# A vision tower's convolution loop with its first activations stored four patches interleaved

## What is computed

```python
x = (x - mean) / (1e-06 + std) / math.sqrt(P)        # per patch and colour
x = _conv2d(x, conv1_w, conv1_b)                     # 3 -> 64 channels, 3x3
residual = x
x = gelu(_group_norm(x, gn1_g, gn1_b))               # 32 groups of 2 channels
x = _conv2d(x, rconv1_w, rconv1_b)                   # 64 -> 64, 3x3
x = gelu(_group_norm(x, gn2_g, gn2_b))
x = _conv2d(x, rconv2_w, rconv2_b)                   # 64 -> 64, 3x3
x = residual + x
x = _conv2d(x, proj_w, proj_b, stride=P, pad=0)      # one token of 192 per patch
```

## Time and profile before

| | us |
|---|---|
| time, median of 3 runs (lowest, highest) | 1486.84 (1485.9, 1489.83) |
| time of the profiled execution | 1486.23 |
| its span | 1484.4 |
| PE busy in it | 1367.0 (92%) |
| DVE busy | 1098.0 (74%) |
| ACT busy | 860.0 (58%) |
| POOL busy | 582.6 (39%) |

### The profile page before, as it was taken

The page is one execution under the profiler, slowest core; times in us unless marked ns, Lnnn a source line. Parts: engine busy times, 40 slices in busy tenths (PEclk is TensorE's granted clock), DMA queues, the critical chain, the costliest instruction groups (busy, mean ns, idle before and its releaser), DMA issues. The chain is left out here.

```text
span 1484.4 us, 43767 instructions
## 1 busy us (share of the span) xinstructions
PE 1367.0 (92%) x14042; PEld 1005.5 (68%) x14042; DVE 1098.0 (74%) x4148; ACT 860.0 (58%) x2126; POOL 582.6 (39%) x1116
## 2 busy tenths in 40 slices
PE   3999988888999999999999998999999977998889
PEld 1865543334888588768977875789588867754647
DVE  4763358999888988888898888888888864545520
ACT  1333337777767776666776766676767630343451
POOL 1000035555554544455455444455454420152600
PEclk9999999999999999999999999999999988898999
DMA  7899845544555555455545554555455579300000
GB/s 209 237 270 267 242 117 160 179 123 128 147 140 134 138 139 147 119 137 146 140 118 156 136 146 104 146 147 139 123 149 139 145 219 259 79 1 1 2 0 17
DMA packets 125141, 205.78 MB, mean 139 GB/s; under 512 B 20028, under 2 KB 88188, under 8 KB 124478
## 3 DMA queue, kind: packets, MB, share of 16 engines
q1 hardware_dynamic: 124990, 203.71, 50.3%
HBM read 103.11 MB, written 20.70 MB: 83 GB/s over the span
## 5 line engine op out<-in xcount | busy, mean ns | idle before, releaser
L629 PE MATMUL rc<-sb_acts,sb_rwd 128*64 128x512 f16 x1764 | 561.5, 391 | 21.4 <-DMA sb_acts<-sb_hst 21.2
L630 PE MATMUL rc<-sb_acts,sb_rwd 128*64 128x512 f16 x1764 | 562.3, 392 | 0.0
L481 POOL TENSOR_TENSOR sb_tmp<-sb_mst,sb_half_neg 128x8 f32<-128x8 f32 x200 | 353.6, 1768 | 463.8 <-DVE sb_mst L956 463.8
L548 ACT ACTIVATE sb_f32q<-c,sb_gsh,sb_gsc 128x128 f32<-128x128 f32 x792 | 298.3, 458 | 274.5 <-POOL sb_gsh L491 274.5
L629 PE MATMUL rc<-sb_acts,sb_rwl 128*64 128x512 f16 x1176 | 362.6, 390 | 5.3 <-issue 5.3
L630 PE MATMUL rc<-sb_acts,sb_rwl 128*64 128x512 f16 x1176 | 362.0, 390 | 0.0
L720 PE MATMUL pj_st<-sb_wall_arena 128*64 128x384 f16 x1792 | 304.0, 333 | 6.6 <-DVE sb_wall_arena L975 6.6
L568 ACT ACTIVATE sb_g2f<-rc,sb_gsh,sb_gsc 128x128 f32<-128x128 f32 x784 | 297.3, 481 | 4.6 <-POOL sb_gsh L491 4.6
L724 PEld LDWEIGHTS pj_st<-sb_wall_arena 128*64 128x64 f16 x1792 | 220.9, 222 | 65.8
L724 PE MATMUL pj_st<-sb_wall_arena 128*64 128x192 f16 x1792 | 240.9, 245 | 0.0
L629 PEld LDWEIGHTS rc<-sb_acts,sb_rwd 128*64 128x64 f16 x1764 | 179.1, 110 | 84.2 <-DMA sb_acts<-sb_hst 33.2
(11 more groups left out here) (190 smaller groups left out, 1864.0 us busy)
## 6 DMA issues: line engine op xcount, KB each, us to landing
sb_acts<-sb_hst SPq DMA_DIRECT2D x792, 78.8 KB, 2.6
sb_im<-x_planes SPq DMA_DIRECT2D x202, 136.5 KB
sb_wall_arena<-w_lo SPq DMA_DIRECT2D x48, 528.0 KB, 3.8
sb_acts<-sb_hst SPq DMA_DIRECT2D x96, 162.0 KB, 3.2
sb_wall_arena<-w_lo SPq DMA_DIRECT2D x24, 480.0 KB, 3.7
sb_f32q<-in_proj SPq DMA_DIRECT2D x12, 576.0 KB, 4.6
sb_wall_arena<-in_proj SPq DMA_DIRECT2D x12, 576.0 KB, 4.6
w_lo<-sb_wall_arena SPq DMA_DIRECT2D x8, 768.0 KB, 3.7
```

The lines of the kernel that those rows point to most:

```text
L481: ch.did(gp.tensor_tensor(t1, var, half_neg[:, :], ALU.pow))
L548: ins = nc.scalar.activation(g1f[:, q * Q + m, :], c1[q][:, m * HALF:(m + 1) * HALF], ACT.Gelu, bias=gsh[q][:, m:m + 1], scale=gsc[q][:, m ...
L629: nc.tensor.matmul(out[0:CH, :], w_odd, x_odd, start=(n == 0), stop=(n == 14))
L630: yield nc.tensor.matmul(out[CH:128, :], w_even, x_even, start=(n == 0), stop=(n == 14))
```

## The change

The four patches of a half are interleaved in `hst` and in `acts`: number by number, four patches side by side, rows of 18 x 4 numbers, as the weight stage has it for channels. A pair's moving operand becomes 8 runs of 64 contiguous numbers, and the shift `m` is four elements. The matmul's output in PSUM then has the patches interleaved as well, so `bn_stats` and `gelu2` of `rc` read every fourth number of a bank (a step of 16 bytes); conv1's input and output stay as they were. `split1` writes its two results with a step of four float16 numbers (8 bytes). The four copies of `double` leave out one zero row of 72 numbers in place of one of 18, so a partition copies 576 numbers (1152 bytes) and not 630 (1260 bytes). `rows_zeroed` clears rows of 72 in place of 18, once. A plane of `acts` grows from 1314 to 1368 numbers (2628 to 2736 bytes), which moves planes 1 and 2 in the weight stage too.

No instruction is added or taken away, and none changes its place on its engine.

```diff
-HB = U * PAD + WD
+HB = U * PAD + WD * Q
@@ double (SP)
-                    sp.dma_start(acts[p][64 * half:64 * half + 64, row, q * Q * PAD + WD:(q + 1) * Q * PAD],
-                                 hst[q][64 * row:64 * row + 64, WD:Q * PAD]).then_inc(s_dup[p][q], 16)
+                    sp.dma_start(acts[p][64 * half:64 * half + 64, row, q * Q * PAD + WD * Q:(q + 1) * Q * PAD],
+                                 hst[q][64 * row:64 * row + 64, WD * Q:Q * PAD]).then_inc(s_dup[p][q], 16)
@@ gelu2_at (ACT)
-                    ins = nc.scalar.activation(g2f[:, q * Q + m, :], rc[p][q][:, m * HALF:(m + 1) * HALF], ACT.Gelu,
+                    ins = nc.scalar.activation(g2f[:, q * Q + m, :], rc[p][q][:, :].rearrange("p (n g) -> p g n", g=Q)[:, m, :], ACT.Gelu,
@@ pairs (PE)
-                    return bass.AP(tensor=buf, offset=k * HB + (q * Q * SL + slot) * WD + m,
-                                   ap=[[3 * HB, 128], [PAD, Q], [WD, 8], [1, P]])
+                    return bass.AP(tensor=buf, offset=k * HB + q * Q * PAD + (slot * WD + m) * Q,
+                                   ap=[[3 * HB, 128], [WD * Q, 8], [1, P * Q]])
@@ rows_zeroed (DVE)
-                    v.memset(t[:, 0:2, q * Q * PAD:q * Q * PAD + WD], 0.0).then_inc(s_rowz, 1)
+                    v.memset(t[:, 0:2, q * Q * PAD:q * Q * PAD + WD * Q], 0.0).then_inc(s_rowz, 1)
@@ channel_stats (DVE)
+                patch = src[:, :].rearrange("p (n g) -> p g n", g=Q) if at else src[:, :].rearrange("p (g n) -> p g n", g=Q)
                 for m in range(Q):
-                    v.bn_stats(bn6[s][:, at + m, :], src[:, m * HALF:(m + 1) * HALF]).then_inc(s_dch, 1)
+                    v.bn_stats(bn6[s][:, at + m, :], patch[:, m, :]).then_inc(s_dch, 1)
@@ split1 (DVE)
-                hi = hst[q][:, :].rearrange("p (g r w) -> p g r w", g=Q, r=SL)[:, :, 1:9, 1:17]
-                lo = acts[p][:, 2, q * Q * PAD:(q + 1) * Q * PAD].rearrange("p (g r w) -> p g r w", g=Q, r=SL)[:, :, 1:9, 1:17]
+                hi = hst[q][:, :].rearrange("p (r w g) -> p g r w", g=Q, r=SL)[:, :, 1:9, 1:17]
+                lo = acts[p][:, 2, q * Q * PAD:(q + 1) * Q * PAD].rearrange("p (r w g) -> p g r w", g=Q, r=SL)[:, :, 1:9, 1:17]
```

## The result

The changed kernel takes 1626.36 us (median of 4 runs, 1622.65 to 1631.04) where the kernel before takes 1486.37 (4 runs on the same chip, 1483.55 to 1489.83): a ratio of **1.093, 95% interval 1.0907 to 1.0952**. It is slower by 140 us; the forecast was 1461.5, the range ended at 1486.

The account below looks back on a forecast made before the run. PE was taken to bound the 144 slots with projection, a ring through DVE, POOL, ACT, DMA and PE the other 52. Terms -21.6 - 2 - 1.5 + 0.5 = -24.6 us took 1486.2 to 1461.5 us, range 1453 to 1486.

Parts of the forecast that it names:

- the 144 slots: Loop slots with projection: PE bounds them at 5.07 us, so a cheaper matmul is worth its full saving there.
- DVE's own slot: Time DVE would need for a loop slot if it waited for nothing: about 4.65 us.
- the other 52: Slots without projection, 4.80 us each: cheaper matmuls worth little (2 us in all), dearer DVE instructions their full cost.
- the ring through five engines: Slots without projection: held by a chain of waits through DVE, POOL, ACT, DMA and PE.
- Part 1, the matmuls: PE's matmuls of pairs: 0.15 us saved a slot (0.10 to 0.19), 21.6 us over 144 slots, mainly from removing odd starts.
- The sum made of it: Whole kernel: -21.6 - 2 - 1.5 + 0.5 = -24.6 us, from 1486.2 to 1461.5 us.
- Two small terms: Further savings: 2 us (0 to 5) in the 52 slots without projection, 1.5 us (0 to 2) in the weight stage.
- with the ends of part 1 alone: Total if only the matmul saving takes its bounds (14.4 to 27 us): stated as 1471 to 1453 us.
- Part 2, DVE: Six DVE instructions a slot get a step: bn_stats stays 283 ns, L966 425, L968 696, no cost.
- The slower rival: PSUM step halves bn_stats' pace: DVE's slot 5.18 us, total 1528 us; chance 0.09 for bn_stats or L968 slower.
- Its last sentence: In split1's TENSOR_TENSOR: the same end, 1528 us, would come if L968's step cost 1.0 ns an element.
- The L966 rival: split1's CAST loses its pace, 0.27 us more: DVE's slot 4.92, 52 slots pay 14 us, total about 1485; chance 0.13.

Follow-up runs that it names:

- e3: The changed kernel with split1 reading and writing contiguously on all sides, values landing at wrong pixels: 1472.25 us, ratio 0.989 to the kernel before.
- e10: The kernel before, with pairs of m = 1 reading where m = 0 reads, so every run starts at an even number: 1478.24 us, ratio 0.991.
- e5: The changed kernel with only split1's CAST writing stepped, its TENSOR_TENSOR contiguous on all sides: 1514.19 us (the kernel before 1491.24).

## Why the prediction was wrong

**The bound.** Right for the 144 slots, and it was the useful part: PE bounds them, DVE's own slot is 4.65 us, and DVE counts as soon as it grows. 4.65 + 1.11 gives the slot that came. For the other 52 the ring through five engines was only part of the story. A slot of group 0 in the kernel before, in which DVE waits for no other engine:

```profile
271.70 0.43 DVE L966 CAST sb_hst<-sb_f32q 128x512 f16<-128x512 f32 x1
...
275.84 0.18 DVE L951 TENSOR_REDUCE sb_mst<-pj_st 128x16 f32<-128x32 f32 x1
...
276.37 0.43 DVE L966 CAST sb_hst<-sb_f32q 128x512 f16<-128x512 f32 x1
```

It takes 4.67 us, the median of group 0; 21 of the 28 distances between CASTs there are 4.70 us or less. So in most of these slots DVE was the bound already, and a saving on PE could not help them.

**Part 1, the matmuls.** The saving of 0.15 us a pass is what e3 shows (2.04 to 1.95 us in nine steps), and its cause is the odd start (e10). The sum made of it was too large. e3, the change with DVE's cost taken out, gives 1.1%, 17 us, not 24.6. Two small terms came to nothing. The weight stage is no shorter (PE busy in 0 to 205 us, first fence; 179.03 before). The slots of group 0 keep their median of 4.67 us, because DVE holds them. In the slots with projection the median falls by 0.13 us, near the 0.15, but the mean by 0.09, from 5.09 to 5.00, because some slots now wait for the copies of `hst` (second fence). The bounds of the sum are added up wrongly as well: "with the ends of part 1 alone" gives 1486.2 - 17.4 = 1469 and 1486.2 - 30 = 1456, not 1471 and 1453. The forecast of 1461.5 itself does not depend on them.

```profile
0.00:205.00 205.00, 179.37 (x1867) 98.76 (x1869) 106.34 (x205) 72.67 (x145) 15.43 (x18) 1.00 0.84 233
```

```profile
L629 PE MATMUL rc<-sb_acts,sb_rwd 128*64 128x512 f16 x1764 | 546.2, 383 | 29.5 <-DMA sb_acts<-sb_hst 28.9
```

The idle time of L629 before those copies was 21.2 us before and is 28.9 in e3. In e10 it is 32.3, with shorter pairs but the old, larger copies. So the new shape of the copies is not needed for the longer waits; that PE, with shorter pairs, arrives earlier fits both. Who makes the copies late was not tested.

**Part 2, DVE: the step that failed.** The prediction says of L968 "with a step of 8 bytes I take no change" and of L966 "I take 425". Measured: +0.81 and +0.43 us of duration, +0.66 and +0.45 of the slot. The reason given for the first was L858, whose results are far apart, too. But L858 writes runs of four float16, whole words, and enters 128 pieces; the changed L968 writes lone ones into 288. It was the nearest row by distance and the wrong one by kind. For L966 the argument was about the pattern's outermost count; that argument was beside the point: CAST still pays half of what TENSOR_TENSOR pays for a piece (2.23 and 4.45 ns), and it was the lone writes that took longer.

**The rivals.** The slower rival was there with a chance of 0.09, on the wrong instruction: `bn_stats` reading PSUM, +0.53 a slot, 1528 us. `bn_stats` didn't change. Its last sentence, that L968's step might cost 1.0 ns an element, was the right place with too small a price: it is 1.6 in the loop by durations (805/512), and CAST's 0.8 comes on top. No case had both together, so no case reached 1626. The L966 rival had the right instruction, size 0.27 for 0.43, and was worth 42 us (e5 over e3), not 23: its price in the 144 slots was set by the share of the gain that it leaves, and it left none.

**The rule on memory lines.** The Trainium skill, "Advanced Engine Details and Errata", Memory Cachelines, was weighed for PSUM only. The runs don't bear it out there for DVE and ACT. The same section's rule for SBUF, lines of 16 bytes and full pace with two hits on each, fits what was read and what was written in whole words (two elements a piece free, one 1.8 ns); it fails for lone float16 writes, where two hits a piece cost 2.2 ns an element and four still just show (731 against 693 ns).

## What to carry to other kernels

When a layout is changed for the engine that bounds, ask of every engine that writes it how many whole words it now writes together, and price that by one instruction measured alone; a row is a neighbour only if it writes the same width in the same way. Let the interleaving happen where results are 4 bytes wide and on an engine with room (here gelu on ACT, 0.12 us for each), so that the narrow writes behind it are contiguous. And before counting a gain on the bounding engine, write down how much the next one may grow: here 0.4 us a slot (5.07 - 4.65) with projection and nothing without, and 1.11 came.

## What the runs showed of the hardware that was not expected

- DVE writing lone float16 results pays 4.45 ns for each 16-byte piece entered (2.2 in a CAST of float32), 4.7 in the loop. Runs of two float16 every 16 bytes, and float32 at a step of 8 bytes, pay nothing (693 ns each). So 512 results take 0.69 us contiguous, 0.73 at a step of 4 bytes, 1.30 to 1.44 at 8 and 2.42 at 16.
- Reads pay only from one element a piece on: 695 ns at a step of 8 bytes, 1064 at 16.
- A step of 16 bytes in PSUM costs DVE's `bn_stats` (299 and 299 ns) and ACT's gelu (457 and 457) nothing.
- A matmul whose moving float16 runs start at an odd element takes some 25 to 30 ns more per 512 columns (0.41 against 0.38 us; 0.15 us over the five such pairs of a pass). The length of the runs (16 in e10, 64 in e3) made no difference that shows: means of 382 and 383 ns.
- A stepped TENSOR_TENSOR of 1.50 us lets the next instruction start after 1.27: its duration overstates what it costs in the slot by 0.23, against 0.08 for the contiguous one.
